# Attention normaliser turned and spread by VectorE, and paired weighings in groups 8 to 14

## The chip, the core and the metric

One core of one Trainium2 chip runs the whole program. The metric is the device time of one execution in microseconds (us). The kernel before takes 1289.16 us, the median of three runs.

## What is computed

A block of a transformer over 2048 tokens of width 512: half a mixture-of-experts layer, attention, half a mixture-of-experts layer, each behind a layer norm. The part that matters here is the causal attention, with 16 heads of 32:

```python
q = apply_rope((x @ wq)...); k = apply_rope((x @ wk)...); v = (x @ wv)...
attn = jnp.einsum('bhqd,bhkd->bhqk', q, k) / np.sqrt(HD)
attn = jnp.where(mask[None, None], -jnp.inf, attn)
attn = jax.nn.softmax(attn, axis=-1)
out = jnp.einsum('bhqk,bhkd->bhqd', attn, v)
return out.transpose(0, 2, 1, 3).reshape(b, t, d) @ wo
```

The softmax's denominator is applied last: the kernel weighs the values with unnormalised exponentials and multiplies the result by one over their sum.

## The kernel before

The program has five stages: first router and experts, projection of q, k and v, attention (span 414 to 1024 us), second router, second experts. Attention runs over 16 **groups** G. A group is one block of 512 queries (b = G // 4) with four heads that share their keys. Groups 0 to 3 have 4 key tiles of 128 keys, groups 4 to 7 have 8, groups 8 to 11 have 12, groups 12 to 15 have 16; the last four tiles of each group are cut by the causal mask. All tiles are numbered through, as n.

For tile n the engines do this:

- TensorE: four **scores** (line 1636), one for each head, from keys and queries, into three banks in turn; score i waits until ScalarE has read score i-3.
- ScalarE: the exponential of each score (line 1755), into one of the P buffers (two in groups 0 to 7, four from group 8 on).
- GpSimd: the mask (line 1814) in the last four tiles; in groups 8 to 14 it also adds some tiles' exponentials together (line 1828).
- TensorE: the **weighing** (line 1648), four products of 32 columns each, one for each head, into bank 3. It stands one tile late: after the four scores of tile n comes the weighing of tile n-1. In tiles whose exponentials nobody else adds, the **sum** with a tile of ones (line 1666) follows, into bank 4; at a group's end the sum of the tiles added elsewhere (line 1657) goes in between.

Between the scores stand the **tops** (line 997): products of queries and keys of later groups, from which VectorE (lines 1010 and 1012) takes each row's maximum. A top waits until VectorE has freed its bank. The tops go round banks 5, 6 and 7; for the groups 7 to 12, from the step called even on, bank 4 is lent to them too, until the first sum of the next group. The tops end at span time 954 us.

At a group's end (step out) ScalarE copies bank 3 to OT (line 1763) and the sums in bank 4 to SM (line 1766). Then the normaliser: TensorE turns SM with four transposes (step **tsum**, line 1674), VectorE takes reciprocals of 16 columns (line 1905), TensorE spreads them again over 128 rows with 16 small products (step **even**, line 1683), and VectorE multiplies OT (line 1915). The steps follow from one list, written by attend_plan, that every engine walks in order: `at` counts scores, tsum is put four scores and even eight scores after out.

```python
                    put(at + 4, ("tsum", G0))
                    put(at + 8, ("even", G0))
```

Beside this, VectorE and ScalarE finish the query blocks (residual, norm, routing) in the groups 5 to 6, 8 to 9 and 12 to 13, with the output projection (line 1703) on TensorE.

Of the kernel before, what the change touches and what calls it, by code (L numbers as in the profile page):

```python
# [216 lines left out]
def memory(nc, ctx, g):  # L217
# [53 lines left out]
    a.R = t("R", [P, 4, 4])  # L271
# [791 lines left out]
def act_found(g, G):  # L1063
    s, act = g.s, g.nc.scalar
    bank, use = g.ring.where[("found", G)]
    act.wait_ge(s(f"full{bank}"), use + 1)
    act_shared(g, ("found", G))
    act.copy(g.mT[:], bk(g, bank)[0:8, :]).then_inc(s(f"free{bank}"), 1)


def act_shared(g, key):

    at = g.shared.index(key)
    if at == 0:
        return
    kind, G = g.shared[at - 1]
    if kind == "found":
        g.nc.scalar.wait_ge(g.s("md"), 16 * G + 16)
    else:
        bank, use = g.ring.where[("tsum", G)]  # L1080
        g.nc.scalar.wait_ge(g.s(f"full{bank}"), use + 1)
# [415 lines left out]

def finish_plan(b):

    todo = [[("proj", b, c)] for c in range(4)]  # L1500
    todo += [[("stats", b, c)] for c in range(4)]
    todo += [[("store", b), ("solve", b)]]
    todo += [[("scale", b, c)] for c in range(4)]
    todo += [[("turn", 4 * b + c)] for c in range(4)]
    return todo + [[("logits", b)], [("best", b)]]


def attend_plan(g):
# [15 lines left out]
    for n, (G, k) in enumerate(TILES):  # L1524
        b = G // 4
        for j in range(4):
# [12 lines left out]
            free = free or any(step[0] == "tsum" for step in due)  # L1539
# [7 lines left out]
            if j == 3 and n:  # L1547
# [3 lines left out]
                plan.append(("weigh", n - 1))  # L1551
                if n - 1 in LAST.values():
                    G0 = TILES[n - 1][0]
                    plan.append(("out", G0))
                    free = False
                    put(at + 4, ("tsum", G0))
                    put(at + 8, ("even", G0))
                    if G0 % 4 == 3:
                        if b == 1:
                            residual(at + 2, 0)  # L1560
                        until = at + (34 if b == 1 else 9)
                        put(until, ("finish", G0 // 4))
                        residual(until + 62, G0 // 4 + 1)
# [8 lines left out]
    plan += [("weigh", len(TILES) - 1), ("out", 15), ("up1", 4), ("split1", 0), ("split1", 1), ("split1", 2), ("split1", 3), ("tsum", 15), ("even", 15)]  # L1572
# [9 lines left out]
    for step in plan:  # L1582
# [13 lines left out]
        if step[0] in ("top", "proj", "tsum", "even", "found"):  # L1596
# [3 lines left out]
        if step[0] == "out":  # L1600
            g.shared.append(("tsum", step[1]))
# [18 lines left out]
def pe_attend(g):  # L1620
# [18 lines left out]
    def weigh(n):  # L1639
# [30 lines left out]
    def tsum(key):  # L1670
        bank = pe_take(g, key)
        pe.wait_ge(s("sm"), key[1] + 1)
        for c in range(4):
            ins = pe.transpose(bk(g, bank)[:, c * P:c * P + P], g.SM[:, c * P:c * P + P], ident)
        ins.then_inc(s(f"full{bank}"), 1)

    def even(key):
        b0, u0 = g.ring.where[("tsum", key[1])]
        pe.wait_ge(s(f"free{b0}"), u0 + 1)
        bank = pe_take(g, key)  # L1680
        for c in range(4):
            for h in range(4):
                ins = pe.matmul(bk(g, bank)[32 * h:32 * h + 32, c * P:c * P + P],
                                a.R[:, c, h:h + 1].to_broadcast([P, HD]), ident, start=True, stop=True)
        ins.then_inc(s(f"full{bank}"), 1)

    def proj(key):
# [4 lines left out]
        b0, u0 = g.ring.where[("even", 4 * b + 3)]  # L1692
        if c == 0:
            b1, u1 = g.ring.where[("even", 4 * b + 2)]
            pe.wait_ge(s(f"free{b1}"), u1 + 1)
        if b == 3:
            pe.wait_ge(s("exp"), 4 * len(TILES))
        if b == 3 and c < 3:
            pe.wait_ge(s("norm"), c + 1)
        else:  # L1700
            pe.wait_ge(s(f"free{b0}"), u0 + 1)
# [4 lines left out]
    for step in g.plan:  # L1706
        kind = step[0]
        if kind == "even" and step[1] in g.lent:
            pe.wait_ge(s("sm"), step[1] + 1)
# [8 lines left out]
        elif kind == "tsum":  # L1718
            tsum(step)
        elif kind == "even":  # L1720
            even(step)
# [12 lines left out]
def act_attend(g):  # L1734
# [22 lines left out]
    def out(G):  # L1757
# [6 lines left out]
        act.wait_ge(s("sum"), SUMMED[LAST[G]] + 1)  # L1764
        act_shared(g, ("tsum", G))
        act.copy(g.SM[:], bk(g, 4)).then_inc(s("sm"), 1)
# [100 lines left out]
def dve_attend(g):  # L1867
    s, dve, a = g.s, g.nc.vector, g.a
# [30 lines left out]
    def tsum(key):  # L1899
        bank, use = g.ring.where[key]  # L1900
        if key[1]:
            b0, u0 = g.ring.where[("even", key[1] - 1)]
            dve.wait_ge(s(f"full{b0}"), u0 + 1)
        dve.wait_ge(s(f"full{bank}"), use + 1)
        dve.reciprocal(a.R[:], bk(g, bank).rearrange("p (c j d) -> p c j d", c=4, j=4)[:, :, :, 0]).then_inc(
            s(f"free{bank}"), 1)

    def even(key):
        G = key[1]
        bank, use = g.ring.where[key]  # L1910
        dve.wait_ge(s(f"full{bank}"), use + 1)
        dve.wait_ge(s("oT"), G + 1)
        o = a.OTs[G // 4 % 2][:, G % 4, :]
        if G < 15:
            dve.tensor_tensor(o, o, bk(g, bank), ALU.mult).then_inc(s(f"free{bank}"), 1)
            return
        for c in range(4):
            v = slice(c * P, c * P + P)
            ins = dve.tensor_tensor(o[:, v], o[:, v], bk(g, bank)[:, v], ALU.mult)
            ins.then_inc(s("norm") if c < 3 else s(f"free{bank}"), 1)  # L1920

    for step in g.plan:
# [8 lines left out]
        elif kind == "tsum":  # L1931
            tsum(step)
        elif kind == "even":
            even(step)
# [217 lines left out]
```

## Time and profile before

| | us |
|---|---|
| three runs | 1288.6, 1289.16, 1290.42 |
| median | 1289.16 |
| the profiled execution | 1283.76 |
| its span, first to last instruction | 1282.5 |
| TensorE busy in the span | 1197.2 (93%) |
| VectorE, ScalarE, GpSimd busy | 893.1, 665.8, 598.1 |
| attention's first score, last score | 414.3, 1013.4 |

The profile comes from a single execution, 5.4 us below the median of the runs. A matmul's row gives its whole way through the array, so rows of TensorE overlap: what one costs the engine is read from the start of one to the start of the next.

### The profile page before, as it was taken

Reading aid. Unit: us, or ns where it says so; the run is one execution under the profiler, and the core shown is the slowest. Engines: PE = TensorE matmul, PEld = TensorE weight load, DVE = VectorE, ACT = ScalarE, POOL = GpSimd, SP = SyncE. Lnnn points to the kernel's source line nnn. Section 1 sums busy time; section 2 is a strip of 40 time slices with the busy share of each in tenths; the row PEclk is TensorE's granted clock in tenths of the full one; section 3 lists DMA queues with packets and bytes.
Section 4 is the critical chain, followed back from the end, with each engine's and each line's share of the span. In section 5 each row is a group of like instructions: output and inputs, shape, how many; then the busy total and the mean of one; then the engine's idle time right before and its main releaser. Section 6 shows DMA issues by size and latency. Waiting matters only on the chain.

```text
span 1282.5 us, 22107 instructions
## 1 busy us (share of the span) xinstructions
PE 1197.2 (93%) x7413; PEld 778.6 (61%) x7413; DVE 893.1 (70%) x2100; ACT 665.8 (52%) x1321; POOL 598.1 (47%) x496
## 2 busy tenths in 40 slices
PE   4899999999998999999999999999999978999996
PEld 3678888858776554445545455545544346777774
DVE  7767777779997665476577677587763666666664
ACT  2545455436555554265466556366567853444442
POOL 4844444313210111001437556455773373888886
PEclk9899999999999999999999999999999999999999
DMA  9923333565530022013445845655743263666665
GB/s 331 365 92 108 112 111 108 172 178 108 98 60 16 21 69 35 1 59 78 98 127 138 165 100 106 192 133 146 152 100 67 84 240 72 106 100 102 101 102 79
DMA packets 68557, 148.52 MB, mean 116 GB/s; under 512 B 8832, under 2 KB 29312, under 8 KB 64448
## 3 DMA queue, kind: packets, MB, share of 16 engines
q0 software_dynamic: 35184, 93.34, 34.1%
q1 hardware_dynamic: 33264, 53.77, 12.1%
q8 instruction: 64, 1.05, 0.3%
q14 instruction: 45, 0.37, 0.1%
HBM read 81.28 MB, written 33.55 MB: 90 GB/s over the span
## 4 chain that ended last, share of the span: by engine, by line
PE 61%; DVE 15%; DMA 10%; issue 6%; POOL 4%; ACT 4%; SPq 0%; POOLq 0%; DVEq 0%; ACTq 0%
PE bank L839 10%; PE bank L1636 10%; PE bank L1648 9%; PE bank L997 8%; PE bank L862 5%; PE bank L1703 4%; PE bank L1666 4%; DMA XG<-xn,TK 3%; DMA out<-Y,DI 3%; POOL out L789 3%; DVE bank L1012 2%; DMA CD<-P 2%; DVE PM L1010 2%; PE bank L821 2%; PE bank L1398 2%
## 5 line engine op out<-in xcount | busy, mean ns | idle before, releaser
L1755 ACT ACTIVATE P<-bank 128x512 f32<-128x512 f32 (+3 forms) x640 | 304.2, 537 | 255.4 <-PE bank L1636 246.2
L1010 DVE TENSOR_REDUCE PM<-bank 128x1 f32<-128x512 f32 x384 | 252.9, 685 | 79.7 <-PE bank L997 78.9
L1636 PE MATMUL bank<-Qs,Ks 98*128 98x512 f32 (+3 forms) x640 | 242.8, 409 | 5.1 <-ACT P L1755 2.8
L997 PE MATMUL bank<-Ks,Qs 96*128 96x512 f32 (+3 forms) x640 | 233.4, 386 | 8.9 <-DVE PM L1012 5.3
L1636 PEld LDWEIGHTS bank<-Qs,Ks 98*128 98x128 f32 x640 | 117.2, 190 | 141.5 <-ACT P L1755 65.3
L1814 POOL TENSOR_SCALAR_AFFINE_SELECT P<-P 128x512 f32<-128x512 f32 x64 | 43.5, 694 | 283.4 <-ACT P L1755 283.4
L1012 DVE CUSTOM_DVE_ANT_0 bank<-bank,KB 128x128 f32<-128x128 f32 (+3 forms) x256 | 124.5, 497 | 51.4 <-PE bank L997 50.7
L1648 PE MATMUL bank<-P,V 128*32 128x512 f32 (+3 forms) x1280 | 151.3, 544 | 4.1 <-POOL P L1814 4.1
L997 PEld LDWEIGHTS bank<-Ks,Qs 96*128 96x128 f32 x640 | 121.7, 191 | 54.1 <-DVE PM L1010 17.0
L1828 POOL TENSOR_TENSOR CH<-CH,P 128x512 f32<-128x512 f32 x108 | 139.5, 1446 | 13.3 <-ACT P L1755 12.7
L789 POOL DMA_INDIRECT out<-Y,DI x78 | 126.3, 1619 | 38.2 <-issue 28.0
L951 DVE TENSOR_TENSOR DL<-W,DH 128x512 fp32r<-128x512 f32 x152 | 98.3, 688 | 41.0 <-issue 21.1
L766 POOL DMA_INDIRECT XG<-xn,TK x78 | 93.5, 1199 | 33.1 <-issue 18.0
L912 ACT CAST DH<-W 128x512 fp32r x152 | 86.7, 618 | 20.3 <-issue 20.3
L839 PE MATMUL bank<-WH,XH 128*128 x312 | 92.4, 418 | 0.9 <-issue 0.6
L839 PE MATMUL bank<-WL,XH 128*128 x312 | 85.7, 396 | 1.5 <-DVE XL L933 1.5
L839 PE MATMUL bank<-WH,XL 128*128 x312 | 85.4, 395 | 0.0
L778 POOL DMA_INDIRECT y<-Y,DI x39 | 38.7, 993 | 96.4 <-DVE Y L961 96.4
L933 DVE TENSOR_TENSOR XL<-bank,XH 128x512 fp32r<-128x512 f32 x78 | 53.9, 691 | 32.8 <-ACT XH L892 28.4
L898 ACT ACTIVATE G<-bank 128x256 f32<-128x256 f32 x78 | 29.9, 384 | 85.0 <-PE bank L839 85.0
L892 ACT CAST XH<-bank 128x512 fp32r<-128x512 f32 x78 | 45.8, 587 | 45.2 <-PE bank L821 42.1
L839 PEld LDWEIGHTS bank<-WL,XH 128*128 128x128 f32 x312 | 58.6, 188 | 16.1 <-issue 1.9
(195 smaller groups left out, 1977.7 us busy)
## 6 DMA issues: line engine op xcount, KB each, us to landing
CD<-P POOLq DMA_DIRECT2D x17, 1024.0 KB, 7.3
xn<-XN SPq DMA_DIRECT2D x8, 1024.0 KB, 6.9
WR<-L_ffn_w POOLq DMA_DIRECT2D x16, 512.0 KB, 15.1
XO<-y POOLq DMA_DIRECT2D x8, 1024.0 KB, 9.6
WR<-L_ffn_w SPq DMA_DIRECT2D x16, 512.0 KB, 7.7
CD<-P SPq DMA_DIRECT2D x7, 1024.0 KB, 5.2
CD<-CH POOLq DMA_DIRECT2D x7, 1024.0 KB, 7.5
XA<-y POOLq DMA_DIRECT2D x24, 256.0 KB, 4.1
```

The costliest lines, as they stand in the source:

```text
L766: pool.indirect_dma_start(out=x.XG[:, j % NG, :], out_offset=None, in_=g.xnd[f][:, :], in_offset=bass.IndirectOffsetOnAxis(ap=r.TK[:, j:j ...
L789: pool.indirect_dma_start(out=g.out.rearrange("t (h d) -> (t h) d", h=2), out_offset=bass.IndirectOffsetOnAxis(ap=r.DI2[:, h, j:j + 1], ax ...
L839: ins = pe.matmul(bk(g, 2 + j % 2), part[:, k * P:k * P + P], w[:, bass.ds(ev[j] * 2048 + k * 512, 512)], start=(n == 0 and k == 0), stop= ...
L912: act.copy(x.DH[:, k, :], W.W3[:, bass.ds(e * 1024 + k * 512, 512)]).then_inc(s("dh"), 1)
L951: ins = dve.tensor_tensor(x.DL[:, k, :], W.W3[:, bass.ds(e * 1024 + k * 512, 512)], DHf[:, k, :], ALU.subtract)
L997: pe.matmul(bk(g, bank)[:, 0:n], g.Qs[b][0:96, G % 4 * 4 + h, c * P:c * P + P], g.Ks[0:96, G % 4, k * BQ:k * BQ + n], start=True, stop=Tru ...
L1010: dve.tensor_reduce(dst, bk(g, bank)[:, 0:n], AX.X, ALU.max).then_inc(s(f"free{bank}"), 1)
L1012: dve.tensor_tensor_reduce(out=bk(g, bank)[:, 0:n], in0=bk(g, bank)[:, 0:n], in1=g.KB[:, CB_MASK + BQ - n:CB_MASK + BQ], scale=1.0, scalar ...
L1636: pe.matmul(bk(g, bank)[:, o:BQ], g.Ks[0:98, G % 4, k * P:k * P + P], g.Qs[G // 4][0:98, G % 4 * 4 + j, o:BQ], start=True, stop=True).then ...
L1648: ins = pe.matmul(bk(g, 3)[32 * h:32 * h + 32, o:BQ], g.V[:, k, q * HD:q * HD + HD], a.P4[buffer_of(n)][:, h, o:BQ], start=(k == 0), stop= ...
L1755: act.activation(a.P4[buffer_of(n)][:, j, o:BQ], bk(g, score_bank(g, i))[:, o:BQ], ACT.Exp, scale=scale).then_inc(s("exp"), 1)
L1828: ins = pool.tensor_tensor(to[:, h, :], two[:, h, :], one[:, h, :], ALU.add)
```

## The change

The normaliser leaves TensorE and ScalarE. At step out VectorE waits for the sums in bank 4 and turns them straight from the bank into SM, in blocks of 32 by 32 (call this T1). One score later it takes 16 reciprocals from SM and turns their broadcast, 128 by 512, back into bank 4 (T2). Three scores after out it multiplies OT by bank 4. ScalarE's copy to SM, the four transposes and the 16 spreading products of TensorE are gone, and two banks' turns in the ring of tops with them.

Bank 4 is therefore in use until the multiplication. TensorE's first sum of the next group waits for it (semaphore even), and where bank 4 is lent to the tops (after groups 7 to 12) TensorE waits for the multiplication at the step even, three scores after out.

The second part: in groups 8 to 14 the weighing of an even tile is held back until the next one's and both stand in a row.

```diff
+def weighed_at(n):
+    if not n:
+        return ()
+    G, k = TILES[n - 1]
+    if G < 8 or G == 15:
+        return (n - 1,)
+    return (n - 2, n - 1) if k % 2 else ()
...
-                plan.append(("weigh", n - 1))
+                plan += [("weigh", m) for m in weighed_at(n)]
...
-                    put(at + 4, ("tsum", G0))
-                    put(at + 8, ("even", G0))
+                    put(at + 1, ("recip", G0))
+                    put(at + 3, ("even", G0))
...
             if fresh and G:
-                pe.wait_ge(s("sm"), G)
+                pe.wait_ge(s("even"), G)
...
         if kind == "even" and step[1] in g.lent:
-            pe.wait_ge(s("sm"), step[1] + 1)
+            pe.wait_ge(s("even"), step[1] + 1)
...
-        act.copy(g.SM[:], bk(g, 4)).then_inc(s("sm"), 1)
...
+    def sums(G):
+        before = shared_before(g, ("sums", G))
+        if before[0] == "found":
+            dve.wait_ge(s("md"), 16 * before[1] + 16)
+        if G:
+            dve.wait_ge(s("even"), G)
+        dve.wait_ge(s("sum"), SUMMED[LAST[G]] + 1)
+        dve.transpose(g.SM[:], bk(g, 4)).then_inc(dv.sem, 1)
+        turned[G] = dv.up()
+
+    def recip(G):
+        dve.wait_ge(dv.sem, turned[G])
+        dve.reciprocal(a.R[:], g.SM[:].rearrange("p (c j) -> p c j", j=32)[:, :, 0]).then_inc(dv.sem, 1)
+        dve.wait_ge(dv.sem, dv.up())
+        dve.transpose(bk(g, 4).rearrange("p (c j) -> p c j", j=32),
+                      a.R[:].unsqueeze(2).to_broadcast([P, 16, 32])).then_inc(dv.sem, 1)
+        spread[G] = dv.up()
```

TensorE where group 10 ends and group 11 begins (in these names bank1 holds bank 3, the weighed values; bank2 holds banks 4 and 5, bank3 banks 6 and 7). Before, the fourth score after out, the turning, the weighing of tile 0, and further on the spreading and the weighing of tile 1:

```order
L1636 MATMUL bank0<-Qs2_135,Ks_137 128x512 [waits exp]
L997 MATMUL bank3<-Ks_137,Qs3_136 128x512 [waits free7]
L1674 MATMUL bank2<-K_49,SM_56 128x128 [waits sm,free5]
L1674 MATMUL bank2<-K_49,SM_56 128x128 x3
L1648 MATMUL bank1<-P40_153,V_138 32x512 [waits oT,exp]
L1648 MATMUL bank1<-P40_153,V_138 32x512 x3
...
L1683 MATMUL bank2<-K_49,R_157 32x128 [waits free4,free5,sm]
L1683 MATMUL bank2<-K_49,R_157 32x128 x15
L1648 MATMUL bank1<-P41_154,V_138 32x512 [waits exp]
L1648 MATMUL bank1<-P41_154,V_138 32x512 x3
```

The same place now, from the third score of the tile to the pair of weighings:

```order
L1643 MATMUL bank0<-Qs2_135,Ks_137 128x512 [waits exp]
L997 MATMUL bank3<-Ks_137,Qs3_136 128x128 [waits free6]
L997 MATMUL bank3<-Ks_137,Qs3_136 128x512 [waits free7]
L1643 MATMUL bank0<-Qs2_135,Ks_137 128x512 [waits exp,even]
L997 MATMUL bank2<-Ks_137,Qs3_136 128x512 [waits free4]
...
L1655 MATMUL bank1<-P40_153,V_138 32x512 [waits oT,exp]
L1655 MATMUL bank1<-P40_153,V_138 32x512 x3
L1655 MATMUL bank1<-P41_154,V_138 32x512 [waits exp]
L1655 MATMUL bank1<-P41_154,V_138 32x512 x3
```

The turning and the spreading are gone, the fourth score after out waits for VectorE's multiplication (even), and tiles 0 and 1 are weighed together.

VectorE at the same place before, from the reciprocal to the multiplication (lines 1010 and 1012 reduce the tops):

```order
L1905 RECIPROCAL R_157<-bank2 128x16 [waits full5,full4]
L1010 TENSOR_REDUCE PM_52<-bank3 128x1 [waits full6]
L1012 ISA bank3,PM_52<-bank3,KB_50 128x256 [waits full7]
L1012 ISA PM_52 128x1
L1010 TENSOR_REDUCE PM_52<-bank2 128x1 [waits full5]
L1010 TENSOR_REDUCE PM_52<-bank3 128x1 [waits full6]
L1010 TENSOR_REDUCE PM_52<-bank3 128x1 [waits full7]
L1915 TENSOR_TENSOR OT0_155<-OT0_155,bank2 128x512 [waits oT,full4]
```

And now, from T1 to the multiplication:

```order
L1888 STREAM_TRANSPOSE SM_56<-bank2 128x512 [waits sum,even,md]
L1010 TENSOR_REDUCE PM_52<-bank3 128x1 [waits full7]
L1893 RECIPROCAL R_157<-SM_56 128x16 [waits dve_chain]
L1895 STREAM_TRANSPOSE bank2<-R_157 128x512 [waits dve_chain]
L1010 TENSOR_REDUCE PM_52<-bank2 128x1 [waits full5]
L1012 ISA bank3,PM_52<-bank3,KB_50 128x128 [waits full6]
L1012 ISA PM_52 128x1
L1010 TENSOR_REDUCE PM_52<-bank3 128x1 [waits full7]
L1904 TENSOR_TENSOR OT0_155<-OT0_155,bank2 128x512 [waits oT,dve_chain]
```

The reductions of four tops and T2 stand between T1 and the multiplication for which TensorE now waits; before, nobody on TensorE waited for it until the bank came up again.

## Rows read from the trace of the kernel before

**Rows 1.** Page, part 1: busy time of each engine, share, instructions.

```profile
PE 1197.2 (93%) x7413; PEld 778.6 (61%) x7413; DVE 893.1 (70%) x2100; ACT 665.8 (52%) x1321; POOL 598.1 (47%) x496
```

**Rows 2.** Windows: length, busy PE, PEld, DVE, ACT, POOL, clock, DMA, GB/s.

```profile
611.40:954.00 342.60, 333.91 (x2138) 177.03 (x2135) 247.90 (x594) 191.91 (x383) 193.57 (x175) 0.99 0.55 132
838.50:848.20 9.70, 9.70 (x55) 5.24 (x51) 9.70 (x21) 6.39 (x12) 9.62 (x9) 1.00 0.41 84
...
942.50:972.00 29.50, 27.26 (x153) 12.10 (x153) 10.47 (x26) 19.95 (x39) 27.83 (x24) 1.00 0.53 109
```

**Rows 3.** Waits, span 400 to 1000: total us, times, longest.

```profile
ACT P L1755 <- PE bank L1636: 243.6, 166, 4.6
```

**Rows 4.** Timeline, TensorE, end of group 10: start, us, form, count.

```profile
758.47 0.43 PE L1648 MATMUL bank<-P,V 128*32 128x128 f32 x8
758.71 1.04 PE L1657 MATMUL bank<-CD,ones 128*32 128x512 f32 x8
759.57 0.40 PE L1666 MATMUL bank<-P,ones 128*32 128x128 f32 x8
759.90 0.50 PE L1636 MATMUL bank<-Qs,Ks 98*128 98x512 f32 x1
...
761.19 0.73 PE L997 MATMUL bank<-Ks,Qs 96*128 96x128 f32 x2
761.76 0.40 PE L1636 MATMUL bank<-Qs,Ks 98*128 98x512 f32 x1
...
762.36 0.60 PE L1674 MATMUL bank<-K,SM 128*128 128x128 f32 x4
762.89 1.07 PE L1648 MATMUL bank<-P,V 128*32 128x512 f32 x8
763.89 0.50 PE L1636 MATMUL bank<-Qs,Ks 98*128 98x512 f32 x1
764.23 0.40 PE L997 MATMUL bank<-Ks,Qs 96*128 96x512 f32 x1
764.47 0.40 PE L1636 MATMUL bank<-Qs,Ks 98*128 98x512 f32 x1
...
766.31 1.08 PE L1683 MATMUL bank<-K,R 128*32 128x128 f32 x32
767.21 1.04 PE L1648 MATMUL bank<-P,V 128*32 128x512 f32 x8
```

**Rows 5.** Timeline, VectorE and ScalarE, same place; in brackets idle before.

```profile
760.68 1.29 DVE L1010 TENSOR_REDUCE PM<-bank 128x1 f32<-128x512 f32 x2 [0.89 <-PE bank L997]
761.88 0.29 DVE L1012 CUSTOM_DVE_ANT_0 bank<-bank,KB 128x128 f32<-128x128 f32 x1
...
763.29 0.24 DVE L1905 RECIPROCAL R<-bank 128x16 f32<-128x16 f32 x1
...
767.46 0.69 DVE L1915 TENSOR_TENSOR OT<-OT,bank 128x512 f32<-128x512 f32 x1
...
760.04 0.58 ACT L1766 COPY SM<-bank 128x512 f32<-128x512 f32 x1 [0.49 <-PE bank L1666]
```

**Rows 6.** Groups of instructions by line: busy us, mean ns, idle before.

```profile
L667 DVE TENSOR_TENSOR LL<-KF,bank 128x1024 f32<-128x1024 f32 x8 | 9.4, 1213 | 0.0
```

**Rows 7.** Timeline, TensorE, group 2: first sum, and the spreading.

```profile
446.88 1.04 PE L1666 MATMUL bank<-P,ones 128*32 128x512 f32 x8
...
449.99 1.08 PE L1683 MATMUL bank<-K,R 128*32 128x128 f32 x32 [0.32 <-DVE PM L1010]
```

**Rows 8.** Timeline, end of attention: the last copy and the multiplication.

```profile
1016.61 0.58 ACT L1766 COPY SM<-bank 128x512 f32<-128x512 f32 x1 [0.49 <-PE bank L1666]
...
1019.53 0.88 DVE L1919 TENSOR_TENSOR OT<-OT,bank 128x128 f32<-128x128 f32 x4 [1.20 <-PE bank L1683]
```

**Rows 9.** Windows on both sides of a fall of the granted clock.

```profile
706.70:710.10 3.40, 1.59 (x14) 0.97 (x11) 1.29 (x2) 1.29 (x4) 3.00 (x4) 1.00 0.59 116
710.10:713.50 3.40, 3.40 (x19) 1.33 (x20) 0.00 (x0) 0.19 (x1) 0.41 (x1) 0.50 1.14 186
```

More of the change, by code:

```diff
@@ L1066, in act_found, with shared_before @@
     act.wait_ge(s(f"full{bank}"), use + 1)
-    act_shared(g, ("found", G))
+    before = shared_before(g, ("found", G))
+    if before and before[0] == "found":
+        act.wait_ge(s("md"), 16 * before[1] + 16)
+    elif before:
+        act.wait_ge(s("even"), before[1] + 1)
     act.copy(g.mT[:], bk(g, bank)[0:8, :]).then_inc(s(f"free{bank}"), 1)
-def act_shared(g, key):
+def shared_before(g, key):
     at = g.shared.index(key)
[L1074 to L1081, printed above, removed]
+    return g.shared[at - 1] if at else None
 def sp_found(g, G):
@@ L1538, in attend_plan @@
             plan += due
-            free = free or any(step[0] == "tsum" for step in due)
+            free = free or any(step[0] == "even" for step in due)
             if turned:
@@ L1595, in attend_plan @@
             ring.set_banks(ids, len(ids) - 1)
-        if step[0] in ("top", "proj", "tsum", "even", "found"):
+        if step[0] in ("top", "proj", "found"):
             ring.take(step)
@@ L1600, in attend_plan @@
         if step[0] == "out":
-            g.shared.append(("tsum", step[1]))
+            g.shared.append(("sums", step[1]))
         elif step[0] == "foundcopy":
@@ L1668, in weigh @@
             ins.then_inc(s("sum"), 1)
[L1670 to L1685, printed above, removed]
     def proj(key):
@@ L1698, in proj @@
         if b == 3 and c < 3:
+            pe.wait_ge(s("even"), 15)
             pe.wait_ge(s("norm"), c + 1)
         else:
[L1701 removed]
+            pe.wait_ge(s("even"), 4 * b + 4)
         for k in range(4):
@@ L1897, in proj_added, with even @@
         dve.wait_ge(s(f"free{bank}"), use + 1)
[L1899 to L1911, printed above, removed]
+    def sums(G):
[14 more added lines that the diff above has]
+        spread[G] = dv.up()
+    def even(G):
+        dve.wait_ge(dv.sem, spread[G])
         dve.wait_ge(s("oT"), G + 1)
@@ L1918, in even @@
             v = slice(c * P, c * P + P)
-            ins = dve.tensor_tensor(o[:, v], o[:, v], bk(g, bank)[:, v], ALU.mult)
-            ins.then_inc(s("norm") if c < 3 else s(f"free{bank}"), 1)
+            dve.tensor_tensor(o[:, v], o[:, v], bk(g, 4)[:, v], ALU.mult).then_inc(s("norm") if c < 3 else s("even"), 1)
     for step in g.plan:
@@ L1930, in dve_attend @@
                 pair(step[1])
-        elif kind == "tsum":
-            tsum(step)
+        elif kind == "out":
+            sums(step[1])
+        elif kind == "recip":
+            recip(step[1])
         elif kind == "even":
-            even(step)
+            even(step[1])
         elif kind == "proj":
```

19 lines of the change are left out of this document (5 added, 14 removed).

## The prediction

> **What bounds the kernel now.** I read the busy shares first: TensorE is busy for 93% of the span, VectorE for 70% [rows 1]. The windows narrow it down: over the groups 8 to 14, as long as there are tops, TensorE is busy for 333.91 of 342.60 us and VectorE for 247.90 [rows 2]. The waits say the same from the other side: ScalarE waits 243.6 us in total for scores, and nobody else is waited for nearly as long [rows 3]. So what TensorE does in attention is on the path. Two places are different. From 838.50 to 848.20 VectorE is busy for 9.70 of 9.70 us beside TensorE, and from 942.50 to 972.00 GpSimd for 27.83 of 29.50 us [rows 2]: there a shorter TensorE has another engine right behind it.
>
> What a step costs TensorE I take from start to start [rows 4]. Score to top in a steady run is 764.47 - 764.23 = 0.24 us. A weighing of 512 columns, eight instructions, lasts 763.89 - 762.89 = 1.00 us, and the score behind it 764.23 - 763.89 = 0.34. Behind another product of 32 columns the same eight instructions last 759.57 - 758.71 = 0.86.
>
> A rule of the Trainium skill speaks against this reading ("Trainium Kernel Development and Optimization", section Performance Expectations): matmul busy time is a bad measure, the busy share of the weight loads a good one. That share is 177.03 of 342.60 us [rows 2]. By the rule TensorE would have half its time free and the sum below would shrink to nothing; the starts, which follow each other at 0.24 us, decide for me against it, and I keep the rule as a rival.
>
> **The change part by part.**
>
> *The normaliser leaves TensorE.* The turning costs 762.89 - 762.36 = 0.53 us and the spreading 767.21 - 766.31 = 0.90 [rows 4], 1.43 us for a group. Groups 0 to 13 have theirs where TensorE sets the pace: 14 x 1.43 = -20.0 us. Group 14's falls into group 15, where there are no tops and ScalarE is the fuller engine; I count only what the copy to SM took of ScalarE, about 0.5: -0.5. Group 15's is on the path with nothing beside it. Before, the copy starts at 1016.61 and the first multiplication at 1019.53 [rows 8], 2.9 us. Now: T1, the reciprocal, T2, 0.69 + 0.28 + 0.69 = 1.7 us: -1.2.
>
> *The price of T1 and T2.* No row of before shows a transpose on VectorE. Other operations on 512 columns last 0.69 us alone (the multiplication) and follow each other at 1.29 - 0.69 = 0.60 (two reductions) [rows 5]. The lower end is therefore 0.6. If every element took two passes, they would cost what 1024 columns cost, 1.21 us [rows 6]. I take 0.69, with 0.60 where the next operation doesn't wait for the result, since all 512-column operations in the rows lie there.
> The Trainium skill ("VectorE: DVE Perf Modes", section The three transpose paths) gives 311 ns for 128 columns in bf16; an estimate from it and 0.96 GHz for 384 columns more is 0.71 us, which would leave the sum as it is.
>
> *Pairs.* A weighing that stands alone pays 1.00 - 0.86 = 0.14, 0.34 - 0.24 = 0.10 on the score behind it and about as much on the way in. Behind another one it saves 0.34 us. Groups 8 to 14 have 24 + 24 = 48 pairs. Five of them lie in group 14 where GpSimd is full [rows 2]: nothing. Of the other 43 I take 30 in full, as VectorE has no room in stretches like 838.50 to 848.20: 30 x 0.34 = -10.2 us.
>
> *The added wait, after groups 7 to 12.* TensorE now stops three scores after out until VectorE has multiplied. At the end of group 10: sums are ready at 760.04, when ScalarE's copy starts [rows 5]. VectorE then does T1 (0.60), a reduction (0.60), the reciprocal (0.28 with its wait), T2 (0.60), a reduction (0.60), a short one (0.29 and its read, 0.35 from start to start), another (0.60) and the multiplication (0.69): 4.3 us, until 764.4. TensorE stands at the fourth score at 761.76 [rows 4]. It waits 2.6 us. Behind the waiting score are queued all scores and tops; ScalarE runs dry after three exponentials, VectorE has no tops left. The other five groups have one or two reductions more or less: 6 x 2.6 = +15.6.
>
> *The added wait, groups 1 to 7.* Here the first sum of the new group waits. In group 2 it starts at 446.88 [rows 7], and would at 446.3 without the turning; by the same addition VectorE is ready at 448.6: 2.3 us. In groups 4 to 7 more tops lie ahead of the sum, and TensorE and VectorE arrive about 0.9 us apart. I take 1.5 on average: 7 x 1.5 = +10.5.
>
> *What these waits take over.* At a group's start TensorE already lost time to VectorE: from the two tops at 761.19 to the score at 761.76 it is 0.57 us where 0.30 would do [rows 4], and in group 2 it waits 0.32 us before the spreading [rows 7]. Three such delays, about 0.8 us, fall into each of the six long waits: -4.8.
>
> *The clock.* Up to 710.1 TensorE was busy for 1.59 of 3.40 us at clock 1.00, and from 710.10 to 713.50 the granted clock was 0.50, that is 1.2 instead of 2.4 GHz [rows 9]. That costs half of 3.4, 1.7 us, where TensorE sets the pace. The new waits make more such thin stretches. Between none and all 13 I take five: +8.5.
>
> *Sum:* -20.0 - 0.5 - 1.2 - 10.2 + 15.6 + 10.5 - 4.8 + 8.5 = -2.1 us. The durations are from an execution of 1283.76 us; the difference is carried to the median: 1289.16 - 2.1 = **1287.0 us**. Its own range is 1281 to 1293, from three falls of the clock more or less and some pairs.
>
> VectorE's load is not the bound by itself: 16 x 2 x 0.6 = 19 us more on 893.1 [rows 1]. The pairs hold tiles back by one, which the four P buffers allow: the next user of a buffer comes one tile after the held weighing. ScalarE is freed of 0.5 us at each group's start, beside other work.
>
> **The rivals.**
>
> *The clock holds.* The waits are there, but the clock falls no more often than before. For it: over the 342.60 us of the groups 8 to 14 the mean clock is 0.99, though TensorE waits many times [rows 2]. Against: 2.6 us is more than the 3.40 - 1.59 = 1.8 us without work in the first window of [rows 9]. 1287.0 - 8.5 = 1278.5 us.
>
> *Slower: every added wait brings the clock down.* The place is the first tile of groups 1 to 13, the price 1.7 us each, so eight more than in my sum: 1287.0 + 13.6 = 1300.6 us. The sum without the clock is -10.6, so from seven falls in all the change is slower than before. For it: the stretch before the known fall had as much work in it as one with a new wait will. Against: in groups 4 to 7 the waits are shorter.
>
> *Transposes at 1.21 us.* Each wait grows by 2 x 0.6: 13 x 1.2 = +15.6, 1302.6 us. For it: nothing but the lack of a row.
>
> *Pairs bring nothing,* because VectorE, with a transpose pair more in each group, sets the pace in the unmasked tiles: +10.2, 1297.2 us. For it: 838.50 to 848.20. Against: 248 of 343 us in the whole.
>
> *The waits are hidden.* VectorE is ready when TensorE comes, since the order of the two is looser than I added it up: -15.6 - 10.5 - 8.5 + 4.8 = -29.8, 1257 us. Against: the multiplication stands behind the top of the same step in VectorE's own order.
>
> *Nothing to gain on TensorE,* a result with which the skill's rule on weight loads would agree: the freed time is idle time, 1289 us. By bounds from the rows it needs the starts at 0.24 us to be paced by somebody else.
>
> **How the numbers follow.** Chances: forecast 0.38; the clock holds 0.20; every wait brings it down 0.15; dear transposes 0.07; pairs nothing 0.10; waits hidden 0.05; nothing to gain 0.05. A measurement tells about 0.2% (2.6 us) from no change: 1286.6 to 1291.7 is the same. Faster: 0.17 of the forecast's 0.38, 0.20 and 0.05, together 0.42. Same: 0.13 of the forecast, 0.05, and 0.02 of the pairs: 0.20. Slower: 0.08 + 0.15 + 0.07 + 0.08 = 0.38. The range 1274 to 1299 leaves out the hidden waits (0.05), the dear transposes (0.07) and half of the falling clock (0.08).
>
> **What the profile after would show.** The lines of turning and spreading gone, 21 us of starts with them. T1 and T2 at 0.69 us. At the starts of groups 8 to 13 an idle stretch of TensorE of 2 to 3 us before a score, put down to VectorE's multiplication, and 1 to 2.3 us before the first sum of groups 1 to 7. Pairs: sixteen instructions of the weighing in 1.00 + 0.86 = 1.86 us. Clock 0.50 for 3.4 us at about five more places. The forecast is wrong if the waits are shorter than 1.5 us (then faster), if the clock falls seven times or more (then slower), or if the time between two weighing blocks is set by VectorE's reductions.

## The result, and the profile after

The changed kernel took 1308.57 us (median, 1306.72 to 1311.8), the kernel before 1289.35 us in the same comparison. The ratio is 1.0169, with a 95% interval from 1.0140 to 1.0197: slower by 1.7%, and outside my range of 1274 to 1299. The profiled execution of the changed kernel took 1308.86 us, with a span of 1307.6 us. That span is 25.1 us longer than the one before, and 22.3 of them lie between the first and the last score of attention. One of e3's four executions below, 1474.65 us at a mean clock of 0.741, is in none of the ratios and means, only in e3's median.

Page of the changed kernel, part 1 and, of part 2, the granted clock in 40 slices:

```profile
PE 1192.0 (91%) x6837; PEld 774.6 (59%) x6837; DVE 911.6 (70%) x2132; ACT 658.9 (50%) x1305; POOL 599.9 (46%) x496
...
PEclk9999999999998999999889899899989999999998
```

TensorE does 576 instructions fewer than in [rows 1], and its share falls from 93% to 91%, but its busy time is nearly the same. A busy microsecond holds less work than before: there are 8s in the row of the clock, and the mean granted clock of the span is 0.967, where the kernel before had 0.988.

The order predicted for the end of group 10 is what stands there now. First TensorE, then VectorE; columns as in [rows 4] and [rows 5].

```profile
769.72 0.40 PE L1673 MATMUL bank<-P,ones 128*32 128x128 f32 x8
770.05 0.50 PE L1643 MATMUL bank<-Qs,Ks 98*128 98x512 f32 x1
...
771.34 0.80 PE L997 MATMUL bank<-Ks,Qs 96*128 96x128 f32 x2
774.53 0.50 PE L1643 MATMUL bank<-Qs,Ks 98*128 98x512 f32 x1 [2.38 <-DVE OT L1904]
774.87 0.40 PE L997 MATMUL bank<-Ks,Qs 96*128 96x512 f32 x1
775.10 0.51 PE L1643 MATMUL bank<-Qs,Ks 98*128 98x512 f32 x1
775.41 0.63 PE L997 MATMUL bank<-Ks,Qs 96*128 96x512 f32 x1
```

```profile
770.29 0.72 DVE L1888 STREAM_TRANSPOSE SM<-bank 128x512 f32<-128x512 f32 x1 [1.21 <-PE bank L1673]
770.93 0.65 DVE L1010 TENSOR_REDUCE PM<-bank 128x1 f32<-128x512 f32 x1
771.51 0.23 DVE L1893 RECIPROCAL R<-SM 128x16 f32<-128x16 f32 x1
771.78 0.73 DVE L1895 STREAM_TRANSPOSE bank<-R 128x512 f32<-128x512 f32 x1
...
773.80 0.68 DVE L1904 TENSOR_TENSOR OT<-OT,bank 128x512 f32<-128x512 f32 x1
```

From T1 (L1888) to the end of the multiplication (L1904) it is 774.48 - 770.29 = 4.2 us, and TensorE waits 2.38 us before its fourth score. Right behind it a full product's duration goes from 0.40 to 0.63 us. That is the clock falling to half.

Everyone who waits for the multiplication in the changed kernel (total us, times):

```profile
L1904 DVE TENSOR_TENSOR OT<-OT,bank x15: 671/679/687, 433.9 to 1007.0; 128x512 f32<-128x512 f32 x15
...
  PEld bank L1643: 17.1, 6
  PE bank L1643: 15.4, 6
  PEld bank L1673: 10.6, 7
  PE bank L1673: 4.3, 5
```

The stretches around three falls of the clock, columns as in [rows 2]; first the start of group 9, then that of group 10, and the last three in group 14.

```profile
679.70:683.10 3.40, 0.56 (x3) 0.32 (x3) 2.98 (x7) 0.20 (x1) 0.00 (x0) 1.00 0.51 202
683.10:686.50 3.40, 3.40 (x10) 2.80 (x9) 2.46 (x6) 2.39 (x4) 1.79 (x2) 0.50 0.00 0
686.50:690.00 3.50, 3.50 (x23) 1.48 (x22) 2.04 (x5) 1.33 (x3) 3.49 (x3) 1.00 0.00 0
```

```profile
727.50:730.90 3.40, 1.07 (x5) 0.51 (x3) 3.37 (x10) 1.46 (x3) 0.07 (x1) 0.99 1.09 343
730.90:734.30 3.40, 3.06 (x7) 2.48 (x8) 2.09 (x4) 1.29 (x3) 1.39 (x2) 0.50 0.27 76
734.30:737.70 3.40, 3.40 (x14) 1.72 (x17) 2.58 (x7) 1.70 (x3) 3.40 (x3) 0.50 1.06 183
737.70:741.10 3.40, 3.40 (x22) 2.01 (x15) 1.44 (x4) 1.67 (x4) 1.40 (x2) 1.00 0.55 101
...
952.70:956.10 3.40, 2.21 (x9) 1.17 (x7) 3.37 (x9) 2.28 (x5) 0.12 (x1) 1.00 0.69 272
956.10:959.50 3.40, 3.06 (x9) 1.69 (x13) 3.08 (x7) 1.38 (x3) 3.40 (x3) 0.51 0.00 0
959.50:962.90 3.40, 3.40 (x17) 0.85 (x10) 0.17 (x1) 0.00 (x0) 1.44 (x2) 0.50 0.01 2
```

The clock falls at thirteen places between the first and the last score, where the kernel before has three. At nine it stays down for 3.4 us, at three for 6.8 and at one for 10.2. In all it is at 0.50 for 61 us of attention, against 10 us in the kernel before. I had foreseen five places more of 3.4 us, 17 us.

Six of the thirteen falls stand at the six waits for the multiplication: the waits end at 621.08, 682.74, 731.24, 774.53, 817.96 and 896.74 us, and the clock falls during them or within 1.4 us of their end, at 621.6, 683.1, 730.9, 775.2, 816.2 and 898.1 us. These six make 34 of the 61 us.

### The profile page after: what moved, and what is told of

The parts are those of the page before. It is cut to its first block, busy times and chain, and to the rows that moved or that the text cites. A ratio compares the mean times of both kernels' runs of the same rounds, so it can differ in the third digit from the quotient of the medians.

```text
span 1307.6 us, 20931 instructions
## 1 busy us (share of the span) xinstructions
PE 1192.0 (91%) x6837; PEld 774.6 (59%) x6837; DVE 911.6 (70%) x2132; ACT 658.9 (50%) x1305; POOL 599.9 (46%) x496
## 4 chain that ended last, share of the span: by engine, by line
PE 55%; DVE 22%; DMA 8%; issue 7%; POOL 4%; ACT 3%; SPq 0%; DVEq 0%; POOLq 0%; ACTq 0%
PE bank L839 9%; PE bank L1655 9%; PE bank L1643 8%; PE bank L997 8%; PE bank L862 5%; DVE PM L1010 4%; PE bank L1690 4%; PE bank L1673 4%; DVE bank L1012 4%; DMA out<-Y,DI 3%; POOL out L789 3%; DMA XG<-xn,TK 3%; PE bank L821 2%; DVE CD L1873 2%; PE bank L1395 2%
## 5 line engine op out<-in xcount | busy, mean ns | idle before, releaser
L1010 DVE TENSOR_REDUCE PM<-bank 128x1 f32<-128x512 f32 x384 | 252.3, 684 | 80.6 <-PE bank L997 79.5
L1643 PE MATMUL bank<-Qs,Ks 98*128 98x512 f32 (+3 forms) x640 | 246.2, 415 | 23.4 <-DVE OT L1904 15.4
L997 PE MATMUL bank<-Ks,Qs 96*128 96x512 f32 (+3 forms) x640 | 245.5, 403 | 16.5 <-DVE PM L1012 6.9
L1643 PEld LDWEIGHTS bank<-Qs,Ks 98*128 98x128 f32 x640 | 121.3, 195 | 129.9 <-issue 68.7
L997 PEld LDWEIGHTS bank<-Ks,Qs 96*128 96x128 f32 x640 | 126.7, 198 | 71.9 <-DVE PM L1010 26.1
L1012 DVE CUSTOM_DVE_ANT_0 bank<-bank,KB 128x128 f32<-128x128 f32 (+3 forms) x256 | 124.4, 497 | 54.0 <-PE bank L997 53.3
L951 DVE TENSOR_TENSOR DL<-W,DH 128x512 fp32r<-128x512 f32 x152 | 98.4, 689 | 41.9 <-ACT DH L912 22.3
L1673 PE MATMUL bank<-P,ones 128*32 128x512 f32 (+3 forms) x664 | 69.4, 490 | 5.1 <-DVE OT L1904 4.3
```

The costliest lines, as they stand in the source:

```text
L951: ins = dve.tensor_tensor(x.DL[:, k, :], W.W3[:, bass.ds(e * 1024 + k * 512, 512)], DHf[:, k, :], ALU.subtract)
L997: pe.matmul(bk(g, bank)[:, 0:n], g.Qs[b][0:96, G % 4 * 4 + h, c * P:c * P + P], g.Ks[0:96, G % 4, k * BQ:k * BQ + n], start=True, stop=Tru ...
L1010: dve.tensor_reduce(dst, bk(g, bank)[:, 0:n], AX.X, ALU.max).then_inc(s(f"free{bank}"), 1)
L1012: dve.tensor_tensor_reduce(out=bk(g, bank)[:, 0:n], in0=bk(g, bank)[:, 0:n], in1=g.KB[:, CB_MASK + BQ - n:CB_MASK + BQ], scale=1.0, scalar ...
L1643: pe.matmul(bk(g, bank)[:, o:BQ], g.Ks[0:98, G % 4, k * P:k * P + P], g.Qs[G // 4][0:98, G % 4 * 4 + j, o:BQ], start=True, stop=True).then ...
L1673: ins = pe.matmul(bk(g, 4)[32 * h:32 * h + 32, o:BQ], g.ones[:], a.P4[buffer_of(n)][:, h, o:BQ], start=fresh, stop=last)
```

## By time and clock, the difference is all in the clock

Each execution comes with its time and its mean granted clock. Within one kernel these two move together: executions of the kernel before went from 1281.58 us at 0.991 to 1291.75 us at 0.981, and the product of time and clock stays at 1270 and 1267 us. I use this product, the time that the kernel would need at full clock, as a second measure. It is an estimate: it treats the whole time as paced by TensorE. But it was 1269.7, 1268.3, 1270.0 and 1270.1 us for the kernel before in the four comparisons that the experiments shared. The product of a single execution scatters by about 2 us (standard deviation), so a difference of 1 or 2 us between two rows says little. The clocks of the kernel before in the comparison with the changed kernel are not on record.

| kernel | time, mean us | mean clock | time x clock | before: time, clock, product |
|---|---|---|---|---|
| changed kernel | 1308.9 | 0.969 | 1268.3 | - |
| e1 normaliser only | 1304.9 | 0.974 | 1270.7 | 1287.2, 0.986, 1269.7 |
| e2 pairs only | 1291.4 | 0.983 | 1269.2 | same |
| e3 lend later | 1301.9 | 0.973 | 1266.4 | same |
| e4 filler | 1297.0 | 0.979 | 1269.8 | same |
| e6 normaliser, no lending | 1290.5 | 0.985 | 1271.2 | 1287.4, 0.985, 1268.3 |
| e7 normaliser, filler | 1290.7 | 0.985 | 1271.6 | same |
| e8 before, no lending | 1296.0 | 0.988 | 1280.1 | same |
| e9 before, VectorE's load | 1301.3 | 0.982 | 1278.2 | same |
| e10 pairs, not the last | 1290.5 | 0.983 | 1268.9 | 1287.4, 0.987, 1270.0 |
| e11 normaliser in five groups | 1284.1 | 0.986 | 1265.5 | same |
| e12 five groups and pairs | 1283.4 | 0.985 | 1264.5 | same |
| e13 filler, pairs not the last | 1294.8 | 0.981 | 1270.2 | 1286.3, 0.987, 1270.1 |

In this measure the changed kernel and the kernel before can't be told apart: 1268.3 us beside 1268.3 to 1270.1. So the question has two halves. Why does the clock fall so much more? And why is 30 us of work taken off TensorE worth nothing at equal clock?

## The experiments

Theory A is my sum with the clock term made larger: the six waits bring the clock down, and all else is as I added it up. Rival B says that the pairs bring nothing, rival C that VectorE's load at the groups' starts holds the tops up. In the expectations from e6 on the names are others: the theory of the clock is C there, and VectorE's load is V.

**e1, the normaliser without pairs; e2, pairs without the normaliser.** e1 is the changed kernel with `weighed_at` giving one tile always; e2 is the kernel before with the new `weighed_at`.

```diff
-    if G < 8 or G == 15:
+    if True:
         return (n - 1,)
```

> The changed kernel with every weighing alone again, as in the kernel before; the normaliser on VectorE and its waits stay. Theory A (the six waits of TensorE at the step even, and the granted clock of 0.50 behind them, cost what was lost, and the pairs gain): about 1315 us, some 7 us above the changed kernel's 1308.6. Rival B (the pairs themselves cost, as TensorE then waits for VectorE's reductions): below 1308.6, near 1300.

> The kernel before, with its normaliser on TensorE, and the weighings of groups 8 to 14 in pairs. Theory A: 10 us faster than before by my sum, 1279 us, and at least 1283. Rival B: no faster than before, 1289 to 1295, with longer waits of TensorE's tops for lines 1010 and 1012 and more stretches at clock 0.50.

e1: 1306.14 us, ratio 1.0146 [1.0104, 1.0188]. e2: 1290.94 us, ratio 1.0035 [1.0016, 1.0055]. The loss comes from the normaliser. The pairs are worth nothing: with them the kernel before was slower by 4 us, and the changed one by some 3, which its intervals alone would not settle. That is rival B, though e1 lies nearer to the changed kernel than the 1300 us that it foretold. The trace of e2 shows why, in TensorE's waits between 640 and 1016 us (total, times, longest). First the kernel before, then e2:

```profile
PE bank L1636 <- ACT P L1755: 2.6, 2, 1.3
PE bank L1059 <- DVE M L1050: 1.7, 3, 1.0
PE bank L997 <- DVE PM L1010: 0.4, 2, 0.3
```

```profile
PE bank L1646 <- ACT P L1765: 5.4, 3, 2.4
PE bank L1059 <- DVE M L1050: 3.5, 3, 1.5
PE bank L997 <- DVE PM L1010: 2.2, 10, 0.3
```

The pair itself does what I had worked out, as this row of e2 shows beside 2 x 1.06 us for two weighings that stand alone:

```profile
647.79 1.92 PE L1658 MATMUL bank<-P,V 128*32 128x512 f32 x16
```

But its time is waited away in three other places: before scores, before the reordering of the maxima (L1059) and before tops, 6.4 us more in all, while the waits of weighings for GpSimd fell by 2.7. The weight loads of the tops wait longer too, 25.0 us for L1010 where the kernel before has 17.0. The largest of TensorE's waits is the score that waits for ScalarE at the start of group 9. ScalarE there changes its function table for a square root (L340) and back, and the exponentials queue behind it; ScalarE and then TensorE in e2:

```profile
663.92 1.28 ACT L340 ACT_TABLE_LOAD   x1
665.21 0.21 ACT L340 ACTIVATE sm<-sm 128x4 f32<-128x4 f32 x1
665.44 1.28 ACT L1765 ACT_TABLE_LOAD   x1
```

```profile
667.06 0.79 PE L1646 MATMUL bank<-Qs,Ks 98*128 98x512 f32 x1 [2.37 <-ACT P L1765]
```

In the kernel before a weighing and its sum, 1.0 us, stand there (663.68 to 664.68), and the wait is 1.33 us:

```profile
666.70 0.50 PE L1636 MATMUL bank<-Qs,Ks 98*128 98x512 f32 x1 [1.33 <-ACT P L1755]
```

So the pair has taken the cover away, and the wait is longer by as much. Behind 2.37 us the product lasts 0.79 us instead of 0.50, for the clock has fallen; in the profiled execution of the kernel before it had not. The cover doesn't explain that part alone. In e1, e6, e7, e8 and e10 below, the same score waits 1.33 to 1.35 us, as in the kernel before, and the clock fell to 0.50 within 2.1 us of the wait's end in each of them.

**e3, bank 4 lent at `at + 8`.** The multiplication has long been done by then, so no score waits for it.

```diff
                     put(at + 3, ("even", G0))
+                    put(at + 8, ("lend", G0))
...
-        if kind == "even" and step[1] in g.lent:
+        if kind == "lend" and step[1] in g.lent:
```

> The changed kernel, but bank 4 is lent to the tops eight scores after out instead of three, and TensorE waits for VectorE's multiplication only there. Theory A: the six waits of 2.4 to 2.8 us are gone and with them most of the time at clock 0.50; 6 x 2.6 + some 15 = about 30 us less than the changed kernel, 1275 to 1282 us. Rival B: only the waits go, 1293 us. Rival C (VectorE's 19 us more of work set the pace at the starts of groups): 1300 us or more, since VectorE's work stays.

1302.78 us, ratio 1.0132 [1.0096, 1.0168]. The six waits for the multiplication are gone, and by the two ratios some 5 us are won, with intervals that overlap. The rest stands before the tops, which have three banks for five scores longer than in the changed kernel. TensorE's waits for the reductions, the changed kernel and then e3:

```profile
PE bank L997 <- DVE PM L1010: 6.0, 18, 0.8
```

```profile
PE bank L997 <- DVE PM L1010: 12.8, 29, 1.0
```

The kernel before has 0.7 us there, and it lends the bank at the same step, eight scores after out. So the bank alone doesn't make these waits; the turns on VectorE and the pairs (2.5 us there in e2) are what e3 has more. And the clock stayed at 0.973: TensorE is at 0.50 for 44 us of attention in the trace of e3, without any of the six long waits. Which waits these falls belong to was not taken apart. I had expected 1275 to 1282 of A; this is rival C's side.

**e4 and e7, filler ahead of the wait.** Ten products that nothing reads stand ahead of each of the six waits. e4 is the changed kernel with them, e7 the same without pairs.

```diff
         if kind == "even" and step[1] in g.lent:
+            pe.wait_ge(s("oT"), step[1] + 1)
+            pe_busy(g, 10)
             pe.wait_ge(s("even"), step[1] + 1)
```

> The changed kernel with ten idle products of 512 columns (about 2.1 us) issued by TensorE ahead of each of the six waits at the step even, after it has seen that bank 3 is copied. They compute nothing that is used. The waits stay as long as they were, only the clock should hold. If the clock is what my sum missed: stretches at 0.50 in the groups 8 to 13 nearly all gone and 12 to 18 us less than the changed kernel, 1291 to 1297 us. If the clock costs little: 1308 us or more.

> The changed normaliser without pairs, with ten products that nothing reads ahead of each of the six waits for the multiplication. The same filler in the whole change gave 1297.6 us. If pairs are worth the 10 us of the prediction while the clock holds, this one stands some 8 to 10 us higher, near 1307; if pairs bring nothing at full clock either, it stands at 1295 to 1299, 7 to 11 us under the normaliser alone (1306.1), with under 25 us of the attention at .50 clock.

e4: 1297.6 us, ratio 1.0087 [1.0054, 1.0120], at the edge of what the theory of the clock expected. e7: 1290.47 us, ratio 1.0022 [1.0003, 1.0040], below both of its expectations. Without pairs the filler gives back 15.7 us of e1's 18.9, and time x clock is unchanged (1270.7 and 1271.6): the work did not become less, the clock came back from 0.974 to 0.985. TensorE at the end of group 10 in e7:

```profile
768.27 0.81 PE L997 MATMUL bank<-Ks,Qs 96*128 96x128 f32 x2
768.92 2.33 PE L378 MATMUL bank<-KB 128*128 128x512 bf16 x10
771.46 0.50 PE L1643 MATMUL bank<-Qs,Ks 98*128 98x512 f32 x1 [0.21 <-DVE OT L1906]
771.79 0.40 PE L997 MATMUL bank<-Ks,Qs 96*128 96x512 f32 x1
772.12 1.06 PE L1655 MATMUL bank<-P,V 128*32 128x512 f32 x8
```

The wait for the multiplication is as long as it was (2.33 + 0.21 us), but the products behind it keep their full speed, 0.40 us for a top and 1.06 for a weighing. It is so at all six places: in the traces of e4 and e7 the clock is 1.00 around each of them. The fifth one, in the changed kernel and in e7 (columns as in [rows 2]):

```profile
816.20:826.40 10.20, 8.45 (x27) 4.06 (x27) 5.64 (x12) 2.98 (x5) 4.97 (x4) 0.50 1.03 343
```

```profile
810.00:835.00 25.00, 24.39 (x99) 11.81 (x100) 15.00 (x32) 8.83 (x16) 12.92 (x11) 1.00 0.80 241
```

In e7 TensorE is at 0.50 for 14 us of attention, in e1 for 48. So most of what the normaliser costs on balance is the clock behind the waits. The waits themselves are still in e7; the work taken off TensorE pays for them. Pairs are at their worst here: with them (e4) the kernel takes 7 us more, at 0.979 instead of 0.985, and at equal clock some 2 us less, which is within the scatter.

**e6 and e8, bank 4 never lent.** e6 is e1 without lending, e8 the kernel before without it.

```diff
-    g.lent, g.back = range(7, 13), {}
+    g.lent, g.back = range(0), {}
```

> The changed normaliser, no pairs, and bank 4 lent to no group: the tops keep three banks through the starts of groups 8 to 13, and TensorE has no wait for the multiplication there. Theory C (the clock, bought by the six waits of 2.1 to 2.8 us): against the kernel before with no lending either, the 20 us of TensorE's work that is gone is a gain, so some 15 to 22 us less than that kernel, with the granted clock at .50 for under 25 us of the attention. Rival V (VectorE's 1.45 us more at each group's start holds the tops up, wherever the bank is): no better than the kernel before without lending, within 5 us of it, and the wait for the tops' reductions (weight load from L1010) 8 us or more above that kernel's.

> The kernel before with bank 4 lent to no group. It prices the fourth bank by itself. If the bank matters as its lending suggests, the reductions of tops hold TensorE longer at the starts of groups 8 to 13: 1 to 2 us for each of six, so 1293 to 1300. If three banks do, 1285 to 1290, and then a change that drops the lending loses nothing.

e6: 1290.93 us, ratio 1.0017 [0.9995, 1.0040]. e8: 1295.90 us, ratio 1.0062 [1.0037, 1.0086]. The fourth bank is worth 8 to 9 us to the kernel before, as expected. Without lending, the new normaliser gains 5 us (e6 against e8), 9 at equal clock. The theory of the clock wanted 15 to 22, rival V no gain, within 5 us, and 8 us more of waiting for L1010. The time lies at V's edge, at equal clock between the two; the waits are V's. The waits of weight loads in e8 and in e6:

```profile
PEld bank L997 <- DVE PM L1010: 25.9, 85, 0.5
```

```profile
PEld bank L997 <- DVE PM L1010: 35.0, 88, 1.3
```

9 us more of waiting for VectorE's reductions, in as many waits. Where bank 4 is lent it is otherwise: there the same wait is 17.0 us in the kernel before, 17.6 with the normaliser alone (e1) and 25.0 with the pairs alone (e2).

```profile
PEld bank L997 <- DVE PM L1010: 17.6, 47, 1.2
```

```profile
PEld bank L997 <- DVE PM L1010: 25.0, 82, 0.7
```

**e9, VectorE's load by itself.** The kernel before with two reductions more in each of 15 groups' starts, which read 512 columns of WO and whose result nothing reads.

```diff
+                    put(at + 1, ("load", G0))
+                    put(at + 3, ("load", G0))
...
+    dve.wait_ge(s("wo"), 16)
...
+            dve.tensor_reduce(a.DY[:], a.WO[:, 0, :].rearrange("p (c j) -> p c j", j=64), AX.X, ALU.max).then_inc(g.dv.sem, 1)
```

> The kernel before with two reductions of 512 columns more on VectorE in each of the first 15 groups' starts, where the change puts its two turns (their result is read by nothing; some 0.6 us each, 1.2 us a group, 18 us in all). Rival V (VectorE's load at the starts holds the tops and through them TensorE): 5 to 15 us slower, 1293 to 1302, with the wait of weight loads for L1010 at 25 us or more where it was 17, and more clock at .50. Theory C (only the six waits for the multiplication count): within 2 us of before, 1286 to 1290.

1301.51 us, ratio 1.0107 [1.0073, 1.0140]. Part of it is of my own making: VectorE has to wait for WO once, before the first top. The added reductions, and that wait:

```profile
L1937 DVE TENSOR_REDUCE DY<-WO x30: 674/678/686, 436.2 to 970.9; 128x8 f32<-128x512 f32 x30
...
DVE PM L1011 <- DMA WO<-L_attn_wo: 8.8, 1, 8.8
```

Group 0 took 5.6 us longer with that. From the first score of group 1 on, up to the last score of all, the profiled execution took 596.4 us where the kernel before took 586.9: 9.5 us for 30 x 0.678 = 20.3 us of VectorE's time. That is 0.47 us for every microsecond put on VectorE. One place more at clock 0.50 is in it, about 1.7 us; without it the share is 0.38. It isn't one accident: eleven of the groups 1 to 14 took 0.4 to 0.6 us longer each, for 1.36 us of reductions at their start. The time is in V's range even without the 5.6 us. The weight loads' wait for these reductions is 26.0 us where it was 17.0, but 4.7 of it is that first wait for WO. The transposes are 16 x (0.716 + 0.727) = 23 us, so by the same share 9 to 11 us of the change is their load, an estimate. My sum had nothing for it.

**e10, pairs without the last pair of each group.**

```diff
-    if G < 8 or G == 15:
+    if G not in (8, 9, 10, 11, 12, 13, 14) or k >= 4 * (G // 4) + 2:
         return (n - 1,)
```

> The kernel before with the pairs of groups 8 to 14, all but the last pair of each group, whose two tiles are weighed one by one as before. With every pair, TensorE waited 2.37 us for an exponential at the start of group 9 (1.33 in the kernel before, where a weighing stands ahead of that score) while ScalarE loaded its tables, and the clock fell behind it. Theory P (a pair costs where the weighing that it takes away covered a wait, at the groups' ends above all): that wait is back to some 1.3 us, no clock fall there, and the kernel takes 1284 to 1288, 3 to 6 us less than with every pair (1290.9). Rival Q (pairs cost everywhere, since tops queue up for VectorE behind 16 instructions of weighing): 1289.5 to 1292, no other than with every pair.

1289.94 us, ratio 1.0025 [1.0004, 1.0045]. The wait that I aimed at did go, as these rows of e10 show: at the start of group 9 it is 1.34 us and the score behind it lasts 0.50. The clock fell there all the same, 1 us later, for 3.4 us where it had been 6.8 in e2 (the last row, columns as in [rows 2]). Another one, in the middle of group 12, stayed at 2.47 (the kernel before has 1.26 there, with a weighing ahead).

```profile
667.17 0.50 PE L1646 MATMUL bank<-Qs,Ks 98*128 98x512 f32 x1 [1.34 <-ACT P L1765]
...
855.83 0.70 PE L1646 MATMUL bank<-Qs,Ks 98*128 98x512 f32 x1 [2.47 <-ACT P L1765]
```

```profile
668.20:671.60 3.40, 3.40 (x20) 1.39 (x22) 2.70 (x6) 1.78 (x4) 0.00 (x0) 0.50 0.00 0
```

The whole gained 1 us against e2, which can't be told from nothing, and not the 3 to 6 of theory P; the waits for VectorE's reductions stayed (25.5 us of weight loads, 25.0 in e2). P was right on the wait and wrong on the clock behind it; Q is nearer to the time.

**e11 and e12, the parts only where they had paid.** The groups' own times in e1, e6 and e7 showed where the new normaliser gained: after groups 0, 2, 6, 13 and 14, where bank 4 is not lent, or few reductions are queued, or (group 14) there are no tops at all. e11 is the kernel before with the new normaliser for these five. e12 adds pairs in groups 8, 10 and 13 without each group's last.

```diff
+BY_VECTOR = (0, 2, 6, 13, 14)
...
-                    put(at + 4, ("tsum", G0))
-                    put(at + 8, ("even", G0))
+                    put(at + (1 if G0 in BY_VECTOR else 4), ("recip" if G0 in BY_VECTOR else "tsum", G0))
+                    put(at + (3 if G0 in BY_VECTOR else 8), ("even", G0))
```

> The kernel before with the changed normaliser in groups 0, 2, 6, 13 and 14 alone, the others as before, and no pairs. By the groups' times of the runs so far these five starts each gained 0.3 to 2.1 us, 4 us together, where the others lost to the wait for bank 4 or to VectorE. Theory D (the gain and the loss are local to each group's start): 1281.5 to 1284.5 beside a before of 1286.7. Rival R (a move in one group shifts the rest, and the clock falls elsewhere): within 2 us of before or above it.

> As the kernel with the normaliser in five groups, and pairs in groups 8, 10 and 13, without each group's last pair; with pairs alone these three groups had taken 1.62, 0.73 and 0.77 us less than before. Theory D with P: 2 to 4 us under that kernel, 1279 to 1282. Rival Q: not under it, 1282.5 or more.

e11: 1284.36 us, ratio 0.9969 [0.9951, 0.9986]. e12: 1283.67 us, ratio 0.9968 [0.9952, 0.9985]. Both are faster than the kernel before by 0.3%, and than the changed one by 2%, by the two ratios. Theory D holds for the normaliser. For the pairs e12 can't be told from e11, and it is outside the 1279 to 1282 of D with P: that is Q.

**e13, filler and pairs without the last.** e4 with e10's condition on `k`.

> The whole change with ten products that nothing reads ahead of each of the six waits for the multiplication, and with the last pair of each group undone, so that a weighing stands again ahead of the score that waits for ScalarE. The time of an execution times its mean granted clock was the same for this change as for the kernel before, within 1 or 2 us of 1269 us, with the pairs or without; if that holds here, the time is 1268 to 1272 us divided by the mean clock, and only the clock can bring it down. Theory K (the clock falls that are left with the filler, mean clock 0.979, belong to the pairs' waits for ScalarE at the groups' ends): mean clock 0.984 to 0.987 and 1286 to 1291. Rival L (they belong to all pairs, or to none): mean clock within 0.002 of 0.979 and 1294 to 1298.

1296.03 us, ratio 1.0074 [1.0053, 1.0096], mean clock 0.981, time x clock 1270.2 us. The product is where it was foretold; the clock is rival L's. The falls that remain with the filler are not those of the last pairs alone. Which pairs they belong to, beyond the one in group 12 (2.46 us there again), stays open.

## Why the prediction was wrong, point by point

I said 1287.0 us from -2.1; it was +19.2. The sum is 21 us short. Its terms beside the runs:

- **The six waits (+15.6) were right.** TensorE waited 15.4 us in six waits for the multiplication, 2.38 at the end of group 10 where I had worked out 2.6. T1 and T2 were right too, 0.716 and 0.727 us for 0.69, and so was the tail: from T1 to the first multiplication 1041.90 - 1040.11 = 1.8 us, for 1.7.
- **The first sums of groups 1 to 7 (+10.5) are open.** They held TensorE's weight loads for 10.6 us, but TensorE itself for only 4.3, and my term meant TensorE.
- **The pairs (-10.2) failed**, by 8 to 10 us at equal clock and by 13 to 14 with the clock. They brought 0.5 us at equal clock in e2, 2.4 in the changed kernel against e1, and the kernel before took 4 us more with them. The step that failed is "of the other 43 I take 30 in full". It asks where VectorE has no room, and never what each held weighing had been covering. My rival "pairs bring nothing", at 0.10, was what happened, though ScalarE's table loads had a part in it beside VectorE. How much each had isn't separated.
- **The clock (+8.5) was too small**, by 7 to 15 us. e1 against e7 puts it at 15.7 us without pairs. The whole change went to 0.969, from 0.985 to 0.987 in the kernel before; 1268.3 us of work over these clocks differs by 21 to 24 us. Both factors of the term failed: ten places more and not five, and I took each to be 3.4 us long, as in [rows 9], where the mean was 61 / 13 = 4.7. The step "between none and all 13 I take five" had no row behind it. The one that I did have spoke for more: the clock fell behind 3.40 us of which 1.8 were without work [rows 9], and each of the six waits was to be 2.6. All six had their fall. From "seven falls in all" on the change should be slower, as I wrote, and it was: the rival "every added wait brings the clock down" at 1300.6 is the nearest, and still 8 us short; it counted the 10.2 us of the pairs as a gain.
- **VectorE's load was missing.** "VectorE's load is not the bound by itself" rests on a mean of 70% [rows 1]. e9 put some 20 us on it and lost 8 to 9.5. The "-4.8 taken over" did not show either: with the normaliser alone (e1) TensorE's waits for the tops' reductions (L1010 and L1012) did not shrink beside the new waits, they went from 6.0 to 10.0 us. Those of weight loads for L1010 grew from 17.0 to 26.1 us in the changed kernel, but that is the pairs' doing: 17.6 in e1, 25.0 in e2.
- **-20.0 for the work off TensorE** can't be seen alone. e6 against e8, with no wait for bank 4 in the groups 8 to 13, is the nearest: 9 us at equal clock. With the first sums' +4 to +10 and VectorE's load of 9 to 11 that adds up to 22 to 30, so the 20.0 may well have been gained and paid away again; no run separates the three. In the groups 1 to 4, where the clock is the same as before, the gain is paid away at once: the changed kernel takes -0.3, +0.1, -0.4 and -0.1 us against the kernel before, though 1.43 us of work are gone from each.

So the steps that failed are three: the gain of the pairs, which was not there; the price of the clock, 8.5 us for at least 15.7; and VectorE's load at the groups' starts, put at nothing, for which e9 gives 9 to 11.

The Trainium skill ("Trainium Kernel Development and Optimization", section Performance Expectations) calls the busy share of the weight loads a good measure of how near TensorE is to its limit. Here it told nothing of the time: PEld went from 778.6 us [rows 1] to 774.6 while the time rose by 19. The estimate for a transpose from the Trainium skill's "VectorE: DVE Perf Modes", section The three transpose paths, 0.71 us, agrees with 0.716 and 0.727.

## What to carry to other kernels

Before pricing a move off a busy TensorE, ask of every added wait not only how long it is but what the granted clock does behind it, and compare executions by time x clock: here it said in one number that the 19 us lost were clock and not work. A step that is held back to stand beside its like was covering something; look at what its old neighbour waits for, above all where another engine changes its table. And an engine at 70% on the mean can still be without room at the places where others begin together, as VectorE was in e9: look for the starts where its queue is short and move work to it there, as e11 does.

## What the runs showed of the hardware

- Executions of one kernel differed by 10 us (1281.58 to 1291.75) with the mean granted clock (0.991 to 0.981), at a constant product.
- The time at 0.50 is not always 3.4 us, as in [rows 9]: it was that behind a stretch with 0.56 us of work in 3.40, but 6.8 us behind one with 1.07, and 6.8 us in group 14 behind one with 2.21, around which TensorE had waited only 0.75 and 0.69 us for reductions. What sets the length stays open.
- With ten products that nothing reads ahead of them, the clock stayed at 1.00 through all six waits of some 2.5 us (e4, e7); without them it fell at all six in the changed kernel. The products take 2.33 us that would have been idle.
- The clock falls at a wait of 1.3 us in some kernels and not in others: at the start of group 9 it fell in e1, e6, e7, e8 and e10, and not in the kernel before. One execution of each was profiled.
- VectorE's transpose of 512 columns in 32-bit takes 0.716 us from PSUM to SBUF and 0.727 us from a broadcast read in SBUF to PSUM, close to any other 512-column operation (0.678 for a reduction).
